# A decoder layer with routed experts: the second normalisation moved to ScalarE, row numbers and totals in one VectorE step, and other orders in the last rounds

## The reference

```python
x = _layernorm(x + _L0_attn_ref(x, ...))                    # self-attention, 2 x 1024 rows of 256
x = _layernorm(x + _L0_xattn_ref(x, ctx_1024, ctx_1024, mask, Wq, Wk, Wv, Wo))   # 16 heads, 64 keys
x = _layernorm(x + _L0_ffn_ref(x, router_w, router_b, w1, b1, w2, b2))
# _L0_ffn_ref: 16 experts, the best 4 of each row
logits = hidden_states @ router_w + router_b
probs = jax.nn.softmax(logits, axis=-1)
topw, topi = jax.lax.top_k(probs, K)
topw = topw / jnp.sum(topw, axis=-1, keepdims=True)
# for each expert: acc + (gelu(x @ w1e + b1e) @ w2e + b2e) * ce[:, None]
```

## Time and profile before

| | |
|---|---|
| median of 3 runs | 593.31 us (590.4 to 594.29) |
| the profiled execution | 599.04 us |
| its span, first to last instruction | 597.3 us |
| busy: TensorE, weight loads | 526.4 us (88%), 494.3 us (83%) |
| busy: VectorE, ScalarE, GpSimd | 409.5 (69%), 333.3 (56%), 283.7 (48%) |
| mean granted TensorE clock | 0.950 |

### The profile page before, as it was taken

One profiled execution on the slowest core, in us unless ns is written; L12 is line 12 of the kernel. 1 busy time (PEld: TensorE's weight loads), 2 busy tenths in 40 slices (PEclk: granted clock), 3 DMA queues, 4 the chain that ended last, 5 costly groups with the idle time before them and its releaser, 6 DMA issues.

```text
span 597.3 us, 14363 instructions
## 1 busy us (share of the span) xinstructions
PE 526.4 (88%) x4028; PEld 494.3 (83%) x4028; DVE 409.5 (69%) x912; ACT 333.3 (56%) x669; POOL 283.7 (48%) x251
## 2 busy tenths in 40 slices
PE   5999999999999989997458999999999999999600
PEld 4988988988988878886258999999999999999500
DVE  2636656566668777775528787888888888788236
ACT  2424333333345555554337788777877878788405
POOL 5550000000015646666600557766677676677624
PEclk9999999999999999998658999999999999999955
DMA  8799999910001313232497999999999999998477
GB/s 271 264 386 385 385 385 386 387 49 0 1 2 49 119 69 114 79 114 89 147 291 270 244 270 254 258 260 262 261 249 261 266 253 268 250 259 201 49 209 235
DMA packets 91834, 127.70 MB, mean 214 GB/s; under 512 B 6736, under 2 KB 62992, under 8 KB 91808
## 3 DMA queue, kind: packets, MB, share of 16 engines
q1 hardware_dynamic: 76320, 107.22, 54.5%
q0 software_dynamic: 14592, 19.93, 16.7%
q10 hardware_dynamic: 896, 0.23, 0.2%
HBM read 62.58 MB, written 64.78 MB: 213 GB/s over the span
## 4 chain that ended last, share of the span: by engine, by line
PE 77%; DVE 6%; issue 4%; DMA 4%; POOL 4%; SPq 1%; ACT 1%; another core or an unknown queue 1%; POOLq 0%; DVEq 0%; ACTq 0%
PE ps L363 19%; PE ps L365 19%; PE ps L364 19%; PE ps L992 3%; POOL expert_rows L584 3%; PE ps L803 2%; PE ps L876 2%; PE ps L839 2%; PE ps L929 1%; PE ps L868 1%; PE ps L860 1%; DMA xg<-expert_rows 1%; DMA x_all<-in_x 1%; PE ps L922 1%; DMA total<-expert_sum 1%
## 5 line engine op out<-in xcount | busy, mean ns | idle before, releaser
L628 POOL DMA_INDIRECT expert_sum<-yb,home_row x80 | 167.9, 2099 | 103.5 <-DVE home_row L1594 82.9
L363 PE MATMUL ps<-gT_h,w_h 128*128 128x256 f32 x320 | 94.9, 296 | 1.9 <-issue 1.3
L363 PE MATMUL ps<-w_h,h_h 128*128 128x256 f32 x320 | 90.7, 283 | 1.2 <-DVE h_l L1587 1.2
L365 PE MATMUL ps<-gT_h,w_l 128*128 128x256 f32 x320 | 91.6, 286 | 0.0
L364 PE MATMUL ps<-gT_l,w_h 128*128 128x256 f32 x320 | 91.5, 286 | 0.0
L364 PE MATMUL ps<-w_l,h_h 128*128 128x256 f32 x320 | 90.6, 283 | 0.0
L365 PE MATMUL ps<-w_h,h_l 128*128 128x256 f32 x320 | 90.5, 283 | 0.0
L584 POOL DMA_INDIRECT expert_rows<-x_all,idx x64 | 63.2, 987 | 27.9 <-issue 21.7
L1587 DVE TENSOR_TENSOR h_l<-hf,h_h 128x1024 fp32r<-128x1024 f32 x40 | 49.0, 1226 | 38.1 <-ACT h_h L1220 36.5
L1213 ACT ACTIVATE hf<-ps,b1s 128x256 f32<-128x256 f32 x160 | 62.9, 480 | 9.2 <-PE ps L365 9.0
L363 PEld LDWEIGHTS ps<-gT_h,w_h 128*128 128x128 f32 x320 | 62.5, 195 | 2.5 <-issue 1.5
(11 more groups left out here) (246 smaller groups left out, 1292.4 us busy)
## 6 DMA issues: line engine op xcount, KB each, us to landing
expert_rows<-zeros SPq DMA_DIRECT2D x32, 1152.0 KB, 14.2
w1f<-in_L_ffn_w SPq DMA_DIRECT2D x40, 512.0 KB
w2f<-in_L_ffn_w SPq DMA_DIRECT2D x40, 512.0 KB
xg<-expert_rows SPq DMA_DIRECT2D x40, 288.0 KB
total<-expert_sum SPq DMA_DIRECT2D x16, 256.0 KB, 5.6
x_all<-in_x SPq DMA_DIRECT2D x8, 256.0 KB, 7.5
expert_sum<-x_all SPq DMA_DIRECT2D x8, 256.0 KB
expert_sum<-total SPq DMA_DIRECT2D x4, 512.0 KB
```

Source lines behind the costliest of these rows:

```text
L363: pe.matmul(o, ah, bh, start=first, stop=False)
L365: return pe.matmul(o, al, bh, start=False, stop=last)
L628: pool.indirect_dma_start(out=sums[p], out_offset=bass.IndirectOffsetOnAxis(ap=home_row[:, p, c:c + 1], axis=0), in_=yb[:, p, c], in_offse ...
```

## The change

x2 is now written by ScalarE: a small VectorE step, `norm_shift`, makes mshift = -mean * rstd, and `norm2` on ScalarE computes Identity(scale * x + bias) with rstd and mshift, first in ScalarE's round. `pos` and `carry` are replaced by one array `taken`, for two tiles in turn, which a single step `rows_of` writes for the row numbers and the totals together; `next_rows` goes. `pipeline` gets a list `ending`, used for rounds 17 to 19, on TensorE, ScalarE and VectorE. GpSimd splits its DMAs in round 17 as 2 + 2 around root2 and in rounds 18 and 19 as 1 + 3.

```diff
@@ pipeline
-        for skew, fn in ramp if t < ramp_steps else stages:
+        for skew, fn in ramp if t < ramp_steps else ending if ending and t > n else stages:
@@ gpsimd
+            def dispatch_half(t, p, k):        # ready, sends 0 and 1; dispatch_other: 2 and 3
...
+            def dispatch_first(t, p, k):
+                ready(t)
+                send(t, p, k, 0)
+
+            def dispatch_rest(t, p, k):
+                for r in range(1, K):
+                    send(t, p, k, r)
-            ending = [(4, dispatch_first), (3, root2), (4, dispatch_rest)]
+            ending = [(4, dispatch_half), (3, root2), (4, dispatch_other)]
+            closing = [(4, dispatch_first), (3, root2), (4, dispatch_rest)]
-                for skew, fn in steady if t < NT + 2 else ending:
+                for skew, fn in steady if t <= NT else ending if t == NT + 1 else closing:
@@ tensor
+                     ending=[(2, cturn_p), (3, turn_o), (4, positions), (3, project), (2, cattend_first), (2, cattend_rest)], unrolled=UNROLLED)
@@ scalar
+            def norm2(t, p, k):
+                act.wait_ge(cshift, done(t))
+                act.activation(halves(x_all[:, ds(p * TPB + tile_of(k), 1), 0:D].rearrange("p a d -> p (a d)")), summed, ACT.Identity,
+                               bias=mshift[:, p:p + 1], scale=rstd[:, p:p + 1]).then_inc(x2, 1)
-            pipeline(act, NT, [(4, neg_max), (4, rexps), (4, top_sum), (3, o_out), (2, p_out), (1, cexps), (2, x1_again), (0, q_out)],
+            pipeline(act, NT, [(4, norm2), (4, neg_max), (4, rexps), (4, top_sum), (3, o_out), (2, p_out), (1, cexps), (2, x1_again), (0, q_out)],
...
+                     ending=[(2, p_out), (4, norm2), (4, neg_max), (4, rexps), (4, top_sum), (3, o_out), (2, x1_again)], unrolled=UNROLLED)
@@ vector
-            def norm2(t, p, k):
+            def norm_shift(t, p, k):
+
                 dve.wait_ge(crst, done(t))
-                dve.tensor_scalar(halves(x_all[:, ds(p * TPB + tile_of(k), 1), 0:D].rearrange("p a d -> p (a d)")), summed, mv[:, p, 0:1], rstd[:, p:p + 1],
-                                  ALU.subtract, ALU.mult).then_inc(x2, 1)
+                dve.wait_ge(x2, freed(t))
+                dve.scalar_tensor_tensor(mshift[:, p:p + 1], mv[:, p, 0:1], -1.0, rstd[:, p:p + 1], ALU.mult, ALU.mult).then_inc(cshift, 1)
...
-                dve.tensor_tensor(pos[:, p], ps[:, 6, D:D + E], carry[:], ALU.add).then_inc(lpos, 1)
-
-            def next_rows(t, p, k):
-                dve.wait_ge(pos_ps, done(t))
-                dve.tensor_tensor(carry[:], ps[:, 6, D + E:D + 2 * E], carry[:], ALU.add).then_inc(lcar, 1)
+                dve.tensor_tensor(taken[:, p], ps[:, 6, D:D + 2 * E].rearrange("p (a e) -> p a e", e=E),
+                                  taken[:, 1 - p, 1].unsqueeze(1).broadcast_to([P, 2, E]), ALU.add).then_inc(lcar, 1)
...
+            ending = [(3, head_inv), (3, head_norm), (4, logits_out), (4, largest), (4, norm_shift), (4, without_top), (4, chosen_mask),
+                      (4, rows_of), (4, chosen_rows), (4, share_sum), (4, slots), (4, all_shares), (4, indices),
+                      (3, stats2), (3, aggr2), (3, var2)]
```

More of the change, by code:

```diff
@@ L85, in score_bank, with pipeline @@
     return 4 if isinstance(t, int) and t == 0 else 2 * p
-def pipeline(eng, n, stages, ramp=None, ramp_steps=0, unrolled=0):
+def pipeline(eng, n, stages, ramp=None, ramp_steps=0, ending=None, unrolled=0):
     depth = max(skew for skew, _ in stages)
@@ L169, in decoder_layer @@
         mhalf = sb("mhalf", [P, 1])
-        carry = sb("carry", [P, E])
+        taken = sb("taken", [P, 2, 2, E])
         x_all = sb("x_all", [P, NT, RW])
@@ L178, in decoder_layer @@
         rstd = sb("rstd", [P, 2])
+        mshift = sb("mshift", [P, 2])
         yres = sb("yres", [P, 2, D])
@@ L249, in decoder_layer @@
         mk = sbe("mk", [P, 2, E], F32R)
-        pos = sbe("pos", [P, 2, E])
         posm = sbe("posm", [P, 2, E])
@@ L520, in _ @@
             pool.wait_ge(c_pool, 20)
-            pool.tensor_scalar(carry[:], iota16[:], float(CAP), 1.0, ALU.mult, ALU.add).then_inc(c_pool, 1)
+            pool.tensor_scalar(taken[:, 1, 1], iota16[:], float(CAP), 1.0, ALU.mult, ALU.add).then_inc(c_pool, 1)
             pool.memset(zeros[:], 0.0).then_inc(c_pool, 1)
@@ L1168, in _ @@
             pipeline(act, NT, [(2, p_high), (4, last_x1_turned), (0, q_high), (1, last_exps)])
[L1170 to L1171 removed]
+            pipeline(act, NT, [(4, norm2), (4, neg_max), (4, rexps), (4, top_sum), (3, o_out), (2, p_out), (1, cexps), (2, x1_again), (0, q_out)],
+                     ramp=[(4, norm2), (4, neg_max), (4, rexps), (4, top_sum), (3, o_out), (2, p_out), (0, q_out), (1, cexps), (2, x1_again)], ramp_steps=RAMP,
+                     ending=[(2, p_out), (4, norm2), (4, neg_max), (4, rexps), (4, top_sum), (3, o_out), (2, x1_again)], unrolled=UNROLLED)
             act.dma_start(b1r[:], b1).then_inc(ld_c, 16)
@@ L1480, in rows_of @@
                 dve.wait_ge(lcar, freed(t) + 1)
-                dve.tensor_tensor(pos[:, p], ps[:, 6, D:D + E], carry[:], ALU.add).then_inc(lpos, 1)
-            def next_rows(t, p, k):
-                dve.wait_ge(pos_ps, done(t))
-                dve.tensor_tensor(carry[:], ps[:, 6, D + E:D + 2 * E], carry[:], ALU.add).then_inc(lcar, 1)
+                dve.tensor_tensor(taken[:, p], ps[:, 6, D:D + 2 * E].rearrange("p (a e) -> p a e", e=E),
+                                  taken[:, 1 - p, 1].unsqueeze(1).broadcast_to([P, 2, E]), ALU.add).then_inc(lcar, 1)
             def chosen_rows(t, p, k):
-                dve.wait_ge(lpos, done(t))
-                dve.tensor_tensor(posm[:, p], pos[:, p], f(mk[:, p]), ALU.mult).then_inc(lpm, 1)
+                dve.wait_ge(lcar, done(t))
+                dve.tensor_tensor(posm[:, p], taken[:, p, 0], f(mk[:, p]), ALU.mult).then_inc(lpm, 1)
             def slots(t, p, k):
@@ L1521, in _ @@
             dve.wait_ge(lcar, done(NT - 1))
-            tstep(dve.scalar_tensor_tensor(cnt[:], iota16[:], -float(CAP), carry[:], ALU.mult, ALU.add))
+            tstep(dve.scalar_tensor_tensor(cnt[:], iota16[:], -float(CAP), taken[:, (NT - 1) % 2, 1], ALU.mult, ALU.add))
             tstep(dve.tensor_tensor(cmp8[:], cnt[:].unsqueeze(2).broadcast_to([P, E, NB]),
```

19 lines of the change are left out of this document (9 added, 10 removed).

## The result

The changed kernel took 602.43 us, median of 4 runs (601.2 to 604.77), the kernel before 592.42 in the same comparison (590.4 to 594.29). The ratio is 1.0166, with a 95% interval from 1.0134 to 1.0198. The change makes the kernel about 10 us slower. The prediction had the direction right and the size wrong: 602.43 lies above its range (589.0 to 600.0), and its chance for this side was 0.12.

The account below looks back on a forecast made before the run. TensorE was taken to bound the rounds, GpSimd's indirect DMAs the stretch past the last scores. Loop +5.2 (6.3 - 1.0) and ending -1.6 gave +3.6 us on 593.31: 596.9 us, range 589.0 to 600.0.

Parts of the forecast that it names:

- waits for oT up to round 16: Rounds 4 to 16: TensorE waits before the positions for a later oT, 4.7 to 6.3 us in sum.
- the last rounds: Rounds 17 to 19, the ending: GpSimd's last send issued at 296.6 instead of 298.02, -1.4 us, rounded to -1.6.
- the give-back: Loop: the octx gap in every second round may swallow new waits, 0 to 2.0 us; the middle, 1.0, was taken.
- oT is just in time: Rounds 5 to 16 except 8: first position product starts 0.14 to 0.15 us after oT's second half ends, hardly any slack.
- 0.57 us later (0.44 to 0.57): ScalarE's round: the new x2 step in front delays the small steps, and oT with them, by this much.
- the mean round from 5 to 16: Sign to look for in the changed profile: about 7.7 us instead of 7.31.
- the signals fall in line: Rival, loop: TensorE's signals come on time, octx gap disappears, rounds 7.23 us, ending -3.0; 589.3 us in all; chance 0.12.
- nothing is given back: Rival, slower: +6.3 us in the loop, 0 in the ending, 599.6 us in all; chance 0.12.
- the rstd of 15 waits for its variance until 287.9: Ending, GpSimd: this rstd ends at 288.4, 1.4 us before the old one, so tile 15's sends follow without a pause.
- One step for rows and totals: VectorE: one 128x32 step for two 128x16, about 0.09 us less; off TensorE's path in the loop, on the chain in round 19.
- VectorE is the hidden bound: Rival: VectorE bounds the rounds, so -4.2 us there and -1.6 in the ending, 587.5 us in all; chance 0.06.

Follow-up runs that it names:

- before, again: The kernel before, unaltered, run and profiled a second time in the second comparison: 592.55 us, ratio 0.9999, profile span 590.5 us.
- the filled kernel: Changed kernel plus 13 transposes of the identity, never read, ahead of tile 0's positions in round 4: 600.69 us, ratio 1.0123 to the kernel before.
- oT second: Changed kernel with ScalarE writing oT right after x2, before the small steps, in all three lists: 606.01 us, ratio 1.0032; again in the third comparison, 591.02 us, 0.9974.

## Why the prediction was wrong, point by point

In the prediction's own terms, with what the profiles after and before, again, show for each (rounds 4 and 5 split by the profile with round 4 filled):

| term | forecast | measured |
|---|---|---|
| waits for oT up to round 16, less what is given back | 6.3 - 1.0, entered as +5.2 | 0.9 + 5.5 = +6.4 |
| TensorE's clock in round 4 | not in the sum | +4.5 |
| the last rounds | -1.6 | +1.0 |
| the rest of the kernel | 0 | -1.0 |
| sum | +3.6 | +10.8 (medians: +10.0) |

Three terms failed: the clock in round 4, put at nothing (4.5 us off in the profiles, 1.5 by the medians of the filled kernel), the gain of the last rounds (2.6 off), and the give-back (1.2 off).

**What was right.** That TensorE bounds the rounds and VectorE does not: x2 off VectorE alone gave 1.0164. That oT is just in time, and that the step in front of it is paid by TensorE. The mechanism was the one forecast, and the size of this term was near: 0.61 us of delay in a round of the loop, just above "0.57 us later (0.44 to 0.57)". The step itself, by groups of the profile after:

```profile
L1141 ACT ACTIVATE x_all<-ps,mshift,rstd 128x256 f32<-128x256 f32 (+1 forms) x16 | 9.0, 564 | 33.1 <-DVE mshift L1459 33.1
```

564 ns, where the nearest form had 593. The Trainium skill (ScalarE: Activation LUTs, What ACT_TABLE_LOAD costs) gives 186 ns and 0.833 ns a column for an instruction with immediate scale and bias and some 93 ns more for each pointer. By that an estimate for 256 columns and two pointers is 585 ns; the trace's 564 comes within 4% of it. The loss by the waits is 5.5 us in rounds 6 to 15 and 0.9 in rounds 4 and 5, where the prediction had up to 6.3 for rounds 4 to 16.

**The give-back, "I take the middle, 1.0", and the base it came from.** The mean round of 7.31 us, the gap before the octx transposes, and the term "I take the middle, 1.0" for what late signals may give back were all read from one execution that stood 5.7 us above the median. The prediction gave that distance, carried the effect over "as it is", and did not ask what the distance consisted of. Against the execution at 592.3, 6.7 us less, it stands in the rounds with the late signals, 73.67 us for rounds 6 to 16 against 68.00, 5.7 more, and in the last rounds, 32.04 against 31.00. That execution, which lies in the middle of the plain runs, has no gap that could swallow anything; its round is 6.80, near the 6.78 that the prediction called clean. Against it the new round of 7.35 is +5.5, with nothing given back. Against the profile ahead of the prediction the same stretch is -0.2. That the loop's +5.2 lies near this +5.5 is luck: it was put together from 6.3 and a give-back of 1.0 that did not occur, over a longer stretch. And the mean round from 5 to 16 did not come at about 7.7 us but at 7.43, the end of the dip included, and at 7.35 from round 6 on.

The rival "the signals fall in line" was right in the profile after, with no late signal and a round of 7.35 (its figure was 7.23), and wrong in its conclusion, since in the kernel before they were in line, too, in the execution at 592.3. The rival "nothing is given back" had the loop right (+6.3) and was nearest for the ending (0); it missed the clock, and so stopped at 599.6.

**The term that was missing: TensorE's clock in round 4.** The prediction followed the exposure "in rounds 4 to 16" and priced round 4 like the others, by the length of the wait. The wait of 1.18 us before tile 0's positions was in the trace, and the clock was thought of only at the end, where it had idled 1.39 us. The wait grew by 0.5 and the granted clock fell to 0.50 for 10.2 us: 4.5 us in the profiles (21.15 against 16.67 with the wait filled), 1.5 in the medians. By the medians this term does not carry the miss alone: the filled kernel, without the dip, is still 8.5 us slower than the kernel before, not 3.6. What is left of the loss with the fill, 600.69 - 592.23 = 8.5 us, is near the sum of the rest, 8.1: 5.5 for rounds 6 to 15, 0.9 for rounds 4 and 5, and 1.7 for the ending, which takes 32.73 us in the filled kernel (266.44 to 299.17) instead of 31.00.

**The ending: "-1.4 us", rounded to -1.6, measured 0.0** (32.01 us from the scores of round 16 to the last indirect DMA after, 298.02 - 265.98 = 32.04 in the profile of the prediction), and +1.0 against the kernel before, again, or +1.8 by the second profile of the changed kernel (32.80). GpSimd after, in its last rounds:

```profile
288.17 0.96 POOL L584 DMA_INDIRECT expert_rows<-x_all,idx  x1 [0.30 <-issue]
292.83 0.95 POOL L584 DMA_INDIRECT expert_rows<-x_all,idx  x1 [3.70 <-DVE idx L1513]
295.04 0.57 POOL L581 TENSOR_TENSOR rstd<-ve,mhalf 128x1 f32<-128x1 f32 x1 [1.25 <-DVE ve L1453]
...
303.46 0.96 POOL L584 DMA_INDIRECT expert_rows<-x_all,idx  x1 [0.30 <-issue]
```

Up to tile 14 the predicted times hold within a microsecond, shifted by the 5.47 us by which round 16 starts later (271.45 - 265.98): the first send of tile 14 forecast at 286.7 + 5.5 = 292.2, measured 292.83. The step that failed is the next one, "the rstd of 15 waits for its variance until 287.9", 293.4 when shifted: it starts at 295.04, 1.7 later, and all seven sends behind it follow without a pause. The wait for oT was forecast: the positions ahead of the projection of tile 15 were to come at 284.65, 290.1 when shifted, and come at 290.42:

```profile
290.42 0.35 PE L945 MATMUL ps<-mk,tri_r 128*128 128x16 f32 x1 [2.62 <-ACT oT L1125]
```

From these positions to the rstd it takes 4.62 us, where the prediction's 284.65 to 287.9 had left 3.25; the granted clock is 0.50 from 288.4 to 319.1. The projection between them alone takes 3.12 us (290.83 to 293.95), where in the profile of the prediction, with a clock of 1.00 there, it took 1.65 (283.05 to 284.70). So the size that was wrong in this step is that of the clock again. With oT second, GpSimd reads:

```profile
276.43 0.96 POOL L584 DMA_INDIRECT expert_rows<-x_all,idx  x1 [0.30 <-issue]
279.53 0.95 POOL L584 DMA_INDIRECT expert_rows<-x_all,idx  x1 [2.14 <-DVE idx L1513]
281.73 0.57 POOL L581 TENSOR_TENSOR rstd<-ve,mhalf 128x1 f32<-128x1 f32 x1 [1.24 <-DVE ve L1453]
...
290.15 0.96 POOL L584 DMA_INDIRECT expert_rows<-x_all,idx  x1 [0.30 <-issue]
```

29.75 us from the scores of round 16 (260.40) to the last send, 1.25 less than the kernel before, again; with x2 on VectorE it is 29.93. Here, too, it is 4.62 us from the positions (277.11) to the rstd; what is won lies ahead of them, since oT is earlier: they start 16.71 us after the scores of round 16, against 18.97 in the changed kernel. So in these profiles the new last rounds, with the one step for rows and totals, hold a gain of 1.1 to 1.25 us, near the forecast 1.4, and only where the write of x2 does not stand with the small steps in front of oT. Two profiles of one kernel differ here by a microsecond (31.00 and 32.04 before, 32.01 and 32.80 changed) and more (29.93 and 34.61 with x2 on VectorE), so this gain is not firm. The clock was dearer, not cheaper: over that stretch the granted clock is 0.71 after and 0.78 before, again, where the prediction had given back 0.2 us for a filled gap. In the times of the changed kernel nothing of the gain can be seen: the old orders there give 1.0178 (1.0147 to 1.0208), the new ones 1.0152 (1.013 to 1.0174), intervals that overlap.

**The rest.** One step for rows and totals was priced at nothing on the path; with the new last rounds it makes 0.9981 (0.9966 to 0.9996), and its own share was not measured. "VectorE is the hidden bound" (587.5) is refuted. The rule of the Trainium skill (Perfetto Trace Analysis, Optimizing Scalar/DVE Operations), that work may go to ScalarE if VectorE is saturated, is not contradicted: VectorE was not saturated, and even with oT in time the move gains nothing that can be told, 0.9974 against 0.9981 with x2 on VectorE, the same within the intervals. No run here has a saturated VectorE.

## What to carry to other kernels

When a step moves to another engine, its place in that engine's queue matters more than its length: the same 0.56 us cost 1.6% ahead of the small steps and oT, and nothing once oT, for which TensorE waits, stood right behind it. The other order, oT ahead of the write of x2, was not tried. Before a trace is used as the base, its distance to the median of the runs has to be explained (here 5.7 us, most of it in rounds with late signals), and terms that live on what only that execution shows are left out. Look in the trace for waits of TensorE that are already long, since one of them, made half a microsecond longer, cost 4.5 us of clock in the profile, and 1.5 us in the medians.

## What the runs showed of the hardware that was not expected

One wait of TensorE, 1.69 us instead of 1.18, in a stretch in which the granted clock had been 1.00, is followed by 10.2 or 10.3 us at 1.2 GHz in the changed kernel and in the move of x2 alone, and, after the same 1.69, by 10.3 us in one and 3.4 us in another execution of the kernel with the old last rounds. Waits of 1.14 and 1.18 at the same place left it at 2.4 GHz in five profiles, and in one, after 1.18, it fell to 1.2 GHz for 3.4 us.

TensorE's signals come late in some executions: 36 to 54 of them by more than 0.1 us within 87 us, and 1.47 us at the place of the earlier trace rows. The kernel before takes 602.05 us on the chip whose profiles show this and 592.2 to 593.0 in the other comparisons, and the move of x2, which costs 1.64% in the third comparison, shows as 0.35% on that chip.
